# Another order of the steps in the attention part of a fused tokenizer, attention and MLP kernel

## The chip, the core and the metric

The kernel runs on one core of a Trainium2 chip. The metric is device time in microseconds (us) of one execution; of several runs the median is given. The engines are called PE (TensorE), DVE (VectorE), ACT (ScalarE), POOL (GpSimd) and SP (SyncE), as the profile calls them.

## What is computed

The reference takes 32 images and 32 texts. Each image is cut into 196 patches of 768 numbers, and the 128 text vectors are put behind them: 324 rows of 256 numbers. Then come causal attention with 16 heads of 16, and an MLP whose inputs and weights are rounded in blocks of 16 to a 4-bit grid (`_GRID`, `_MID`). Cut to what matters:

```python
h = patches @ W.T + b                      # 32 x 196 x 256
h = concatenate([h, txt], axis=1)          # 32 x 324 x 256
# attention: q, k, v of layernorm(h), 16 heads
att = softmax(where(mask, q @ k.T * 0.25, -inf))
h = h + (att @ v) @ Wo + bo
# MLP: fp4_linear quantises its input and its weight blockwise
x = layernorm(h)
h = h + fp4_linear(silu(fp4_linear(x, w_gate)) * fp4_linear(x, w_up), w_down)
```

## The kernel before

The kernel has two parts, one after the other. `phase_a` does the embedding, the attention and the quantising of the MLP's input and weights; `phase_b` does the MLP on 81 tiles of 128 rows. The change is in `phase_a` alone.

`phase_a` is a software pipeline over images, written by hand. `pipeline` runs `body(k)` for iterations -1 to 34 on every engine. In iteration n the kernel embeds image n+1 (`tok`, `h0`, `root`, `xn shift`, `xn`), makes q, k and v of image n (`xnT`, `qk`, `v`, `rest`, `part 1`, `last`), takes the row maxima of the scores of image n-1 (`MAX_A` for heads 0 to 7, `MAX_B` for heads 8 to 15, seven steps each) and its first two groups of exponentials (`exp 0`, `exp 1`), finishes the attention of image n-2 (`exp 2`, `exp 3`, `attend`, `turn`, `turnback`, `proj`), and normalises and quantises image n-3 (the steps that begin with `x2`). One of 33 pieces of the MLP's weights is quantised by nine small VectorE steps, `w 0` to `w 8`.

The list `STEPS` gives the order. Every engine walks through the same list and does its share of each step, in this order; instructions of an engine run strictly one behind the other, and between engines there are only semaphores. So a step's place in the list sets what it stands behind on each engine. Things that the steps below turn on:

- A score matmul for the maxima writes the PSUM tensor `maxp`, and VectorE's maximum (line 605) frees it. The scores for the exponentials go to `expp`, which ScalarE's exponential (line 828) frees. There is one of each. `linA` and `linB` are taken in turn by `xnT`, `qk`, `v`, `turn`, `turnback` and `proj`; `attp` is shared by `attend` and `neg`.
- `neg` transposes the maxima on TensorE (line 955) into `attp`, VectorE splits them into three bf16 parts (lines 616 to 623), and `neg out` sends them by three transfers from ScalarE's queue into rows of `qst` (line 816). `exp 0 0` waits for those of `neg 0`, and `exp 2 0` of the next iteration for those of `neg 1`.
- `w 7` is `w_y<-w_y,w_m` (line 663), a VectorE operation with both inputs in SBUF. `patches` copies the next patches (line 559), and GpSimd forms the low part in `patches lo` (line 54). `root` is GpSimd's power (lines 512 and 515), from which VectorE forms `xshift` (line 737) and ScalarE the normalised rows `xn` (line 843), which TensorE transposes in `xnT` at the start of the next iteration (line 911).
- `rest` (line 484) and `last` (line 490) are GpSimd's subtractions for the second and third bf16 part of q and k. SyncE stacks the parts into `qst` and `kst` with twelve transfers (line 426), which the next iteration's first scores wait for. The third part of k follows `last 1`. GpSimd also masks the exponentials (line 507), and `attend` waits for the mask.

Of the kernel before, what the change touches and what calls it, by code (L numbers as in the profile page):

```python
# [142 lines left out]
STEPS = [
    ("h0b",), MAX_A[0], ("x2 stats",), ("xnT", 0), ("attend", 1, 0), ("exp", 2, 0), MAX_A[1], ("xnT", 1), ("tok", 1),
    ("exp", 2, 1), ("attend", 1, 1), ("x2 root",), MAX_A[2], ("w", 0), ("exp", 2, 2), ("x2 shift",), ("qk", 0),
    MAX_A[3], ("exp", 2, 3), ("x2 norm",), ("attend", 1, 2), ("w", 1), ("tok", 1), MAX_A[4], ("rest", 0), ("tok", 1),
    ("x2 scale",), ("qk", 1), ("exp", 3, 0), MAX_A[5], ("qk", 2), ("attend", 2, 0), ("x2 y",), ("attend", 2, 1),
    ("attend", 2, 2), ("exp", 3, 1), ("x2 sq",), MAX_A[6], ("w", 2), ("tok", 1), ("w", 3), ("rest", 1), ("tok", 1),
    ("exp", 3, 2), ("neg", 0), ("neg out", 0), ("qk", 3), MAX_B[0], ("exp", 3, 3), ("attend", 3, 0), ("tok", 2),
    ("x2 t",), MAX_B[1], ("tok", 2), ("part 1", 0), ("w", 4), ("x2 q",), ("tok", 1), ("x2 out",), ("exp", 0, 0),  # L150
    MAX_B[2], ("tok", 1), ("exp", 0, 1), ("w", 5), ("attend", 3, 1), ("attend", 3, 2), MAX_B[3], ("exp", 0, 2),
    ("turn", 0), ("turn", 1), ("tok", 1), ("exp", 0, 3), ("part 1", 1), ("h0",), ("turn", 2), ("root",),
    ("exp", 1, 0), ("attend", 0, 0), ("last", 0), ("v", 0), ("exp", 1, 1), MAX_B[4], ("turnback", 0), ("v", 1),
    MAX_B[5], ("patches",), ("attend", 0, 1), ("w", 6), ("turnback", 1), ("attend", 0, 2), ("last", 1), MAX_B[6],
    ("patches lo",), ("w", 7), ("exp", 1, 2), ("v", 2), ("xn shift",), ("neg", 1), ("neg out", 1), ("proj", 0),
    ("xn",), ("exp", 1, 3), ("w", 8), ("proj", 1),
]
# [1224 lines left out]
```

## Time and profile before

| | us |
|---|---|
| median of 3 runs | 2053.52 (2045.04 to 2055.91) |
| time of the profiled execution | 2044.34 |
| span of the profiled execution | 2042.5 |
| PE busy (share of the span) | 1781.4 (87%) |
| DVE busy | 1627.8 (80%) |
| ACT busy | 961.4 (47%) |
| POOL busy | 872.1 (43%) |

The span is what the trace covers, 1.8 us less than the time of the same execution. Busy time counts instructions and no waiting.

### The profile page before, as it was taken

Reading aid. Unit: us, or ns where it says so; the run is one execution under the profiler, and the core shown is the slowest. Engines: PE = TensorE matmul, PEld = TensorE weight load, DVE = VectorE, ACT = ScalarE, POOL = GpSimd, SP = SyncE. Lnnn points to the kernel's source line nnn. Section 1 sums busy time; section 2 is a strip of 40 time slices with the busy share of each in tenths; the row PEclk is TensorE's granted clock in tenths of the full one; section 3 lists DMA queues with packets and bytes.
Section 4 is the critical chain, followed back from the end, with each engine's and each line's share of the span. In section 5 each row is a group of like instructions: output and inputs, shape, how many; then the busy total and the mean of one; then the engine's idle time right before and its main releaser. Section 6 shows DMA issues by size and latency. Waiting matters only on the chain. (4 is left out here: it accounts for less than half of the span.)

```text
span 2042.5 us, 37905 instructions
## 1 busy us (share of the span) xinstructions
PE 1781.4 (87%) x14552; PEld 1471.4 (72%) x14552; DVE 1627.8 (80%) x3188; ACT 961.4 (47%) x1646; POOL 872.1 (43%) x971
## 2 busy tenths in 40 slices
PE   3698888988888888888888888887499999999998
PEld 3477666776666766666776676664389999999997
DVE  5667788777887778877788787875399999999998
ACT  1255555555555555455554565554233333333333
POOL 5445555555555555555555555552012121121211
PEclk8899999899998999999999899997699999999999
DMA  3544554445544455444554445540211111111111
GB/s 104 92 70 71 91 87 94 81 71 90 88 90 85 71 88 87 86 93 71 87 91 86 89 71 88 78 75 21 66 52 58 58 57 60 58 60 58 60 58 47
DMA packets 140650, 152.45 MB, mean 75 GB/s; under 512 B 20279, under 2 KB 135607, under 8 KB 140471
## 3 DMA queue, kind: packets, MB, share of 16 engines
q1 hardware_dynamic: 133558, 149.02, 37.4%
q8 instruction: 117, 1.92, 0.4%
q10 hardware_dynamic: 6912, 1.00, 0.3%
q14 instruction: 63, 0.51, 0.1%
HBM read 51.25 MB, written 34.01 MB: 42 GB/s over the span
## 5 line engine op out<-in xcount | busy, mean ns | idle before, releaser
L605 DVE TENSOR_REDUCE maxima<-maxp 108x2 f32<-108x648 f32 (+2 forms) x448 | 415.6, 928 | 235.9 <-PE maxp L946 235.8
L828 ACT ACTIVATE probs<-expp 108x648 f32<-108x648 f32 (+2 forms) x512 | 363.7, 710 | 271.0 <-PE expp L971 257.3
L507 POOL TENSOR_SCALAR_AFFINE_SELECT probs<-probs 108x216 f32<-108x216 f32 (+1 forms) x512 | 286.4, 563 | 381.1 <-ACT probs L828 380.2
L1189 POOL TENSOR_TENSOR hq<-q_b,scale_b 128x704 f32<-128x704 f32 x81 | 112.6, 1390 | 471.0 <-DVE q_b L1246 471.0
L943 PE MATMUL maxp<-kst,qst 96*108 96x108 bf16 (+2 forms) x1536 | 279.6, 275 | 18.3 <-DMA kst<-parts 10.8
L971 PE MATMUL expp<-qst,kst 99*108 99x324 bf16 (+2 forms) x1536 | 251.8, 274 | 44.2 <-DMA qst<-negparts 33.8
L943 PEld LDWEIGHTS maxp<-kst,qst 96*108 96x108 bf16 x1536 | 179.1, 137 | 71.4 <-issue 23.5
L971 PEld LDWEIGHTS expp<-qst,kst 99*108 99x108 bf16 x1536 | 151.1, 134 | 106.4 <-DMA qst<-negparts 43.4
L992 PE MATMUL attp<-probs,vblk 108*32 108x324 f32 (+2 forms) x3072 | 223.2, 388 | 2.5 <-POOL probs L507 1.5
L946 PE MATMUL maxp<-mask_qk,identb 108*108 108x108 bf16 (+2 forms) x896 | 222.8, 255 | 0.0
L59 PE MATMUL gu<-wgu_hi,xqT_hi 128*128 128x512 f32 (+1 forms) x486 | 191.4, 394 | 2.0 <-DVE xqT_lo L1201 2.0
L484 POOL TENSOR_TENSOR rest<-qkf,parts 128x648 f32<-128x648 f32 x64 | 95.3, 1489 | 227.8 <-ACTq L801 227.8
L60 PE MATMUL gu<-wgu_lo,xqT_hi 128*128 128x512 f32 (+1 forms) x486 | 183.8, 378 | 0.0
L61 PE MATMUL gu<-wgu_hi,xqT_lo 128*128 128x512 f32 (+1 forms) x486 | 183.6, 378 | 0.0
L1272 ACT ACTIVATE hqT_hi<-turn_h 128x768 fp32r<-128x768 f32 x81 | 66.0, 815 | 199.2 <-PE turn_h L1339 199.2
L59 PE MATMUL tokp<-wtok_hi,patches_hi 128*88 128x256 f32 (+1 forms) x384 | 132.1, 344 | 19.1 <-POOL patches_lo L54 19.1
L843 ACT ACTIVATE xn<-h,xshift,rstd 108x256 f32<-108x256 f32 x96 | 50.6, 590 | 185.7 <-issue 175.1
L992 PEld LDWEIGHTS attp<-probs,vblk 108*32 108x32 f32 x3072 | 73.0, 113 | 75.1 <-issue 40.0
L946 PEld LDWEIGHTS maxp<-mask_qk,identb 108*108 108x108 bf16 x896 | 121.6, 136 | 1.2
L490 POOL TENSOR_TENSOR parts<-rest,parts 128x648 bf16<-128x648 f32 x64 | 113.0, 1766 | 0.0
L1262 ACT ACTIVATE silu_b<-gu 128x704 f32<-128x704 f32 x81 | 61.8, 763 | 108.2 <-PE gu L61 108.2
L60 PE MATMUL tokp<-wtok_lo,patches_hi 128*88 128x256 f32 (+1 forms) x384 | 112.5, 293 | 0.0
(183 smaller groups left out, 4499.6 us busy)
## 6 DMA issues: line engine op xcount, KB each, us to landing
qst<-parts SPq DMA_DIRECT2D x192, 162.0 KB, 5.1
kst<-parts SPq DMA_DIRECT2D x192, 162.0 KB, 5.9
patches<-in_xT SPq DMA_DIRECT2D x32, 588.0 KB, 4.6
h_dram<-h_rows SPq DMA_DIRECT2D x32, 324.0 KB
xq_dram<-x_n SPq DMA_DIRECT2D x32, 324.0 KB
xq<-xq_dram SPq DMA_DIRECT2D x81, 128.0 KB, 2.0
res<-h_dram SPq DMA_DIRECT2D x81, 128.0 KB, 2.1
out_rows<-ot SPq DMA_DIRECT2D x81, 128.0 KB, 1.7
```

The source lines that it names most:

```text
L59: pe.matmul(dst, a[0], b[0], start=start, stop=False)
L60: pe.matmul(dst, a[0], b[1], start=False, stop=False)
L61: return pe.matmul(dst, a[1], b[0], start=False, stop=stop)
L490: pool.tensor_tensor(parts[:, 2, t], rest[:, t], parts[:, 1, t], ALU.subtract).then_inc(part_done[2], 1)
L507: pool.affine_select(out=at, in_=at, compare_op=ALU.is_ge, fill=0.0, base=0, pattern=[[0, nh], [1, CH]], channel_multiplier=-1).then_inc(p ...
L605: dve.tensor_reduce(rowmax[half][:, h:h + nh, c].rearrange("p (a h) -> p a h", a=2), src, AX.X, ALU.max).then_inc(maxp_free, 1)
L828: act.activation(dst, expp[0:CH, 0:banks, 0:per * w], ACT.Exp, scale=SCALE).then_inc(expp_free, 1)
L943: pe.matmul(maxp[0:CH, a, x * w:(x + 1) * w], qst[other][0:ROWS, h, c * CH:(c + 1) * CH], kst[other][0:ROWS, h, 0:w], start=x == 0, stop=F ...
L946: ins = pe.matmul(maxp[0:CH, a, 0:per * w].rearrange("p (h w) -> p h w", w=w)[:, :, w - CH:w], identb[0:CH, 0:CH], mask_qk[:].unsqueeze(1) ...
L971: ins = pe.matmul(expp[0:CH, a, x * w:(x + 1) * w], kst[s][0:ROWS + NPART, h, kc * CH:(kc + 1) * CH], qst[s][0:ROWS + NPART, h, kc * CH:T] ...
L992: ins = pe.matmul(attp[VW * x:VW * (x + 1), kc * CH:T], v_of[:, kc, 4 * q + x, :], probs[:, q, lo:lo + T - CH * kc], start=kc == 0, stop=k ...
L1189: pool.tensor_tensor(blocks(hq[t % 2][:, 0:FF]), blocks(q[:]), spread(scale[:], P, NB_H), ALU.mult).then_inc(hq_done, 1)
```

## The change

Only the list `STEPS` changes. The same steps stand in it, each once, in another order.

```diff
 STEPS = [
-    ("h0b",), MAX_A[0], ("x2 stats",), ("xnT", 0), ("attend", 1, 0), ("exp", 2, 0), MAX_A[1], ("xnT", 1), ("tok", 1),
...
+    ("x2 stats",), MAX_A[0], ("tok", 1), ("x2 root",), ("xnT", 0), ("attend", 1, 0), ("exp", 2, 0), MAX_A[1],
...
-    ("patches lo",), ("w", 7), ("exp", 1, 2), ("v", 2), ("xn shift",), ("neg", 1), ("neg out", 1), ("proj", 0),
-    ("xn",), ("exp", 1, 3), ("w", 8), ("proj", 1),
+    MAX_B[6], ("exp", 1, 2), ("attend", 0, 2), ("v", 2), ("w", 6), ("neg", 1), ("xn",), ("neg out", 1), ("w", 7),
+    ("proj", 0), ("w", 8), ("proj", 1), ("exp", 1, 3),
 ]
```

What this does to the engines is seen in their instructions. First VectorE, near the end of an iteration in the middle of the program, from the copy of the patches on. Before:

```order
L559 CAST patches_hi<-patches 128x1176
L661 SCALAR_TENSOR_TENSOR w_y<-w_y,w_m 128x128
L54 TENSOR_TENSOR attnT_lo<-linA,attnT_hi 128x324
L605 TENSOR_REDUCE maxima<-maxp 108x2
L663 TENSOR_TENSOR w_y<-w_y,w_m 128x128
L629 TENSOR_TENSOR vblk<-linB,bv 108x16x16
L737 SCALAR_TENSOR_TENSOR xshift<-meanvar,rstd 108x3
L616 TENSOR_SCALAR negparts<-attp 24x108
L618 SCALAR_TENSOR_TENSOR negrest<-attp,negparts 24x108
L621 CAST negparts<-negrest 24x108
L623 TENSOR_TENSOR negparts<-negrest,negparts 24x108
L596 TENSOR_TENSOR h_rows<-linA,h0b 108x512
```

And after the change, the same place, from `xn shift` on:

```order
L737 SCALAR_TENSOR_TENSOR xshift<-meanvar,rstd 108x3
L54 TENSOR_TENSOR attnT_lo<-linA,attnT_hi 128x324
L605 TENSOR_REDUCE maxima<-maxp 108x2
L629 TENSOR_TENSOR vblk<-linB,bv 108x16x16
L661 SCALAR_TENSOR_TENSOR w_y<-w_y,w_m 128x128
L616 TENSOR_SCALAR negparts<-attp 24x108
L618 SCALAR_TENSOR_TENSOR negrest<-attp,negparts 24x108
L621 CAST negparts<-negrest 24x108
L623 TENSOR_TENSOR negparts<-negrest,negparts 24x108
L663 TENSOR_TENSOR w_y<-w_y,w_m 128x128
L596 TENSOR_TENSOR h_rows<-linA,h0b 108x512
```

`w 7` (line 663) stood ahead of the last eviction of v, of `xshift` and of the maxima's parts, and now stands behind them all; `xshift` has moved ahead of the last maximum.

GpSimd, from `root` (lines 512 and 515) to the next iteration's first masks. Before:

```order
L512 TENSOR_TENSOR vareps<-meanvar,eps 108x3
L515 TENSOR_TENSOR rstd<-vareps,minus_half 108x3
L507 AFFINE_SELECT probs<-probs 108x2x108
L490 TENSOR_TENSOR parts<-rest,parts 128x648
L507 AFFINE_SELECT probs<-probs 108x2x108
L490 TENSOR_TENSOR parts<-rest,parts 128x648
L54 TENSOR_TENSOR patches_lo<-patches,patches_hi 128x1176
L507 AFFINE_SELECT probs<-probs 108x4x108
L507 AFFINE_SELECT probs<-probs 108x432
L529 TENSOR_TENSOR h0b<-h_1,bo 108x768
```

And after, from `last 0` (line 490) on:

```order
L490 TENSOR_TENSOR parts<-rest,parts 128x648
L512 TENSOR_TENSOR vareps<-meanvar,eps 108x3
L515 TENSOR_TENSOR rstd<-vareps,minus_half 108x3
L54 TENSOR_TENSOR patches_lo<-patches,patches_hi 128x1176
L507 AFFINE_SELECT probs<-probs 108x2x108 x2
L490 TENSOR_TENSOR parts<-rest,parts 128x648
L507 AFFINE_SELECT probs<-probs 108x4x108
L507 AFFINE_SELECT probs<-probs 108x432
L519 TENSOR_TENSOR x_vareps<-x_meanvar,eps 108x3
```

`patches lo` (line 54) has moved from behind `last 1` to right behind `root`, ahead of `last 1`; `h0b` (line 529) no longer stands here but some masks into the next iteration.

ScalarE, from the exponential that `exp 1 2` issues at the end of an iteration. Before:

```order
L828 ACTIVATE probs<-expp 108x864
L816 DMA qst<-negparts 1x24x108 x3
L843 ACTIVATE xn<-h_1,xshift,rstd 108x256 x3
L828 ACTIVATE probs<-expp 108x432
L784 ACTIVATE xnT_hi<-linA 128x324
```

And after:

```order
L828 ACTIVATE probs<-expp 108x864
L810 ACTIVATE attT<-attp 128x324
L843 ACTIVATE xn<-h_1,xshift,rstd 108x256 x3
L816 DMA qst<-negparts 1x24x108 x3
L828 ACTIVATE probs<-expp 108x432
L784 ACTIVATE xnT_hi<-linA 128x324
```

The rows `xn` now stand ahead of the three transfers, and the copy of `attend 0`'s result (line 810) has come in behind the exponential.

In the first half of the iteration `qk 3` has moved ahead of `neg 0` and two `tok` steps behind it, `x2 norm` stands ahead of `exp 3 0` as before, `x2 t` (line 707) stands right behind the maxima's parts of `neg 0` and ahead of `MAX_B[0]`, and `h0b` stands behind `MAX_A[4]`. SyncE's list is not written by `STEPS`, but each of its transfers waits for a step: the texts' for `h0b`, the stacks' for `exp 3 3`, `part 1` and `last`.

## Rows read from the trace of the kernel before

**Rows 1.** Windows of the execution: each engine's busy time, TensorE's granted clock, DMA.

```profile
80.00:1400.00 1320.00, 1150.62 (x10541) 902.34 (x10540) 1031.03 (x2170) 712.57 (x1261) 713.26 (x835) 0.93 0.47 82
...
1470.00:2042.00 572.00, 560.98 (x3564) 513.10 (x3564) 523.09 (x893) 215.16 (x325) 112.59 (x81) 0.99 0.18 56
```

**Rows 2.** TensorE's timeline: start, length, line, tile, count, [idle <- releaser].

```profile
143.71 0.47 PE L911 MATMUL linA<-ident,xn 108*128 108x108 f32 x3 [2.58 <-ACT xn L843]
...
1293.21 0.78 PE L911 MATMUL linA<-ident,xn 108*128 108x108 f32 x3 [2.66 <-ACT xn L843]
...
1332.90 0.47 PE L911 MATMUL linA<-ident,xn 108*128 108x108 f32 x3 [1.39 <-ACT xn L843]
```

**Rows 3.** TensorE's timeline from 713 to 763 us.

```profile
713.77 0.28 PE L955 MATMUL attp<-ident,maxima 108*128 108x108 f32 x1
...
720.18 0.48 PE L971 MATMUL expp<-qst,kst 99*108 99x324 bf16 x2 [1.05 <-DMA qst<-negparts]
...
736.04 0.37 PE L59 MATMUL linB<-wo_hi,attnT_hi 128*108 128x256 f32 x1 [1.24 <-DVE vblk L629]
...
740.41 0.77 PE L911 MATMUL linA<-ident,xn 108*128 108x108 f32 x3 [2.65 <-ACT xn L843]
...
742.36 0.79 PE L971 MATMUL expp<-qst,kst 99*108 99x324 bf16 x2
...
745.15 0.44 PE L971 MATMUL expp<-qst,kst 99*108 99x324 bf16 x2
...
762.38 0.48 PE L971 MATMUL expp<-qst,kst 99*108 99x324 bf16 x2 [1.05 <-DMA qst<-negparts]
```

**Rows 4.** VectorE's timeline near 732 us, and line 663's minimum, median, maximum (ns).

```profile
731.88 0.83 DVE L605 TENSOR_REDUCE maxima<-maxp 108x2 f32<-108x648 f32 x1
...
732.62 3.04 DVE L663 TENSOR_TENSOR w_y<-w_y,w_m 128x128 f32<-128x128 f32 x1
...
L663 DVE TENSOR_TENSOR w_y<-w_y,w_m x33: 276/3030/3534, 29.2 to 1366.6; 128x128 f32<-128x128 f32 x33
```

**Rows 5.** Timelines of VectorE (first row) and GpSimd (the others).

```profile
730.60 0.76 DVE L559 CAST patches_hi<-patches 128x1176 fp32r<-128x1176 f32 x1
...
727.75 0.85 POOL L515 TENSOR_TENSOR rstd<-vareps,minus_half 108x3 f32<-108x3 f32 x1
...
728.91 1.42 POOL L490 TENSOR_TENSOR parts<-rest,parts 128x648 bf16<-128x648 f32 x1
...
730.62 2.23 POOL L490 TENSOR_TENSOR parts<-rest,parts 128x648 bf16<-128x648 f32 x1
...
732.81 2.70 POOL L54 TENSOR_TENSOR patches_lo<-patches,patches_hi 128x1176 fp32r<-128x1176 f32 x1
```

**Rows 6.** ScalarE's timeline and queue, and two of its grouped lines (500 to 1300 us).

```profile
714.38 2.27 ACTq L816 DMA_DIRECT2D qst<-negparts  x3
...
731.11 0.44 ACT L810 ACTIVATE attT<-attp 128x324 f32<-128x324 f32 x1
...
731.96 0.89 ACT L828 ACTIVATE probs<-expp 108x864 f32<-108x864 f32 x1 [0.41 <-PE expp L971]
...
736.30 2.28 ACTq L816 DMA_DIRECT2D qst<-negparts  x3
...
738.69 1.58 ACT L843 ACTIVATE xn<-h,xshift,rstd 108x256 f32<-108x256 f32 x3 [5.83 <-issue]
...
L828 ACT ACTIVATE probs<-expp 108x648 f32<-108x648 f32 (+2 forms) x300 | 213.1, 710 | 152.4 <-PE expp L971 146.9 <-issue 0.4
...
L795 ACT ACTIVATE qkf<-linB,bqk 128x324 f32<-128x324 f32 x37 | 19.7, 532 | 37.9 <-issue 37.7
```

**Rows 7.** SyncE's queue: the last stack transfer; TensorE: the first scores behind it.

```profile
732.88 0.55 SPq L426 DMA_DIRECT2D kst<-parts  x1
...
736.84 0.36 PE L943 MATMUL maxp<-kst,qst 96*108 96x108 bf16 x4
```

**Rows 8.** A window of two microseconds, columns as in the first group.

```profile
738.00:740.00 2.00, 0.00 (x0) 0.00 (x0) 2.00 (x5) 1.31 (x3) 0.00 (x0) 0.56 0.30 87
```

More of the change, by code:

```diff
@@ L143 @@
 STEPS = [
-    ("h0b",), MAX_A[0], ("x2 stats",), ("xnT", 0), ("attend", 1, 0), ("exp", 2, 0), MAX_A[1], ("xnT", 1), ("tok", 1),
[L145 to L153, printed above, removed]
@@ L154 @@
-    MAX_B[5], ("patches",), ("attend", 0, 1), ("w", 6), ("turnback", 1), ("attend", 0, 2), ("last", 1), MAX_B[6],
-    ("patches lo",), ("w", 7), ("exp", 1, 2), ("v", 2), ("xn shift",), ("neg", 1), ("neg out", 1), ("proj", 0),
-    ("xn",), ("exp", 1, 3), ("w", 8), ("proj", 1),
+    ("x2 stats",), MAX_A[0], ("tok", 1), ("x2 root",), ("xnT", 0), ("attend", 1, 0), ("exp", 2, 0), MAX_A[1],
+    ("xnT", 1), ("attend", 1, 1), ("exp", 2, 1), ("attend", 1, 2), MAX_A[2], ("x2 shift",), ("exp", 2, 2), ("qk", 0),
@@ new lines @@
+    MAX_A[3], ("tok", 1), ("exp", 2, 3), ("w", 0), ("x2 norm",), ("tok", 1), ("w", 1), MAX_A[4], ("h0b",),
+    ("x2 scale",), ("exp", 3, 0), ("qk", 1), ("qk", 2), MAX_A[5], ("x2 y",), ("exp", 3, 1), ("attend", 2, 0),
+    ("rest", 0), ("qk", 3), MAX_A[6], ("w", 2), ("attend", 2, 1), ("attend", 2, 2), ("x2 sq",), ("exp", 3, 2),
+    ("neg", 0), ("x2 t",), ("neg out", 0), ("tok", 1), ("rest", 1), MAX_B[0], ("tok", 1), ("exp", 3, 3), ("tok", 2),
+    ("tok", 2), ("part 1", 0), MAX_B[1], ("attend", 3, 0), ("tok", 1), ("x2 q",), ("exp", 0, 0), ("w", 3), ("w", 4),
@@ new lines @@
+    MAX_B[2], ("tok", 1), ("exp", 0, 1), ("x2 out",), ("attend", 3, 1), ("w", 5), ("attend", 3, 2), MAX_B[3],
+    ("exp", 0, 2), ("turn", 0), ("tok", 1), ("h0",), ("exp", 0, 3), ("v", 0), ("turn", 1), ("last", 0), ("root",),
+    ("patches",), ("patches lo",), ("part 1", 1), ("attend", 0, 0), ("exp", 1, 0), MAX_B[4], ("turn", 2),
+    ("exp", 1, 1), ("v", 1), MAX_B[5], ("turnback", 0), ("last", 1), ("xn shift",), ("turnback", 1), ("attend", 0, 1),
+    MAX_B[6], ("exp", 1, 2), ("attend", 0, 2), ("v", 2), ("w", 6), ("neg", 1), ("xn",), ("neg out", 1), ("w", 7),
```

## The prediction

> **What bounds the kernel now.** I began with the windows [rows 1]. The MLP part, from 1470 us on, has TensorE busy 561 of 572 us, and the change doesn't touch it. In the attention part TensorE is busy 1151 of 1320 us, VectorE 1031, at a mean granted clock of 0.93: no engine is full, so a chain of waits sets the time. The transposes at the start of an iteration give its period: from 143.71 to 1293.21 us there are 27 periods, 42.57 us each [rows 2].
>
> Then I followed TensorE through one iteration [rows 3]. I count from the first scores of `exp 0 0`, at 720.18. The next landmark is `exp 2 0` at 742.36, 22.2 us later, and the next `exp 0 0` comes at 762.38, 20.0 us later still. TensorE idles 1.05 us for the transfers of the maxima's parts, 1.24 us for the last eviction of v, and 2.65 us for the rows `xn`. Behind the last two its clock falls: it is granted 0.56 in the window from 738 us [rows 8], between its two levels of 1.2 and 2.4 GHz. The steps from 742.36 to 745.15 take 2.8 us; the same four steps at full clock take about 1.5 us by the pitch of such steps later in this trace (my estimate).
>
> Both waits have one source [rows 4]. Line 663 takes 3.04 us at 732.62, where its shortest instance takes 0.28, and the median of 33 is 3.03. While it stands there GpSimd runs `patches lo`, 2.70 us from 732.81 [rows 5]. Behind line 663 on VectorE are the eviction of v, `xshift` and the maxima's parts. Behind those parts on ScalarE's queue are the three transfers, 2.28 us of issue, and only then `xn` at 738.69 [rows 6]. That is the chain of the idle 2.65 us.
>
> One iteration near the end of the pipeline shows what its absence is worth: the one that ends at 1332.90 has no patches to load, so no `patches lo`. Its wait for `xn` is 1.39 us in place of 2.66, and its period is 39.69 [rows 2], 2.9 under the mean. It also leaves out the copy of the patches, so not all of this is the collision.
>
> The Trainium skill (SBUF — State Buffer, "SBUF: two separate sides") has a rule for this: a VectorE operation with two SBUF inputs, or in a 2-port mode, and a GpSimd operation exclude each other for a whole instruction. By that rule the trace agrees, with 3.04 us against 0.28.
>
> **The change, part by part: second half of the iteration.** Time T runs from `exp 0 0`. VectorE has nearly the same set of steps before the last maximum as before, so that maximum still begins at about T = 11.7 (731.88 less 720.18) [rows 3, 4]. Likewise the exponential of `exp 1 2` begins at about 11.8 (731.96) and takes 0.89, to 12.7. Behind it now stands the copy of `attend 0` (0.44), which frees `attp` at 13.1 [rows 6]. `neg 1` needs that tensor, so it can't transpose before 13.1, although the maxima are there at 12.5. Line 663 is behind it, where GpSimd has only masks: it should take 0.3 us, not 3.0, and nothing on the path stands behind it but the residuals.
>
> `xn` runs on ScalarE from 13.1 to 14.6 (1.58) [rows 6]. TensorE has `proj 0`, `proj 1`, `exp 1 3`, the first maxima and one `tok` before it needs `xn`, about 3.9 us by the pitch of these steps at full clock, so it asks at 17 or later: the wait for `xn`, 2.65 us now, goes. What is late next are the transfers of `neg 1`. They now stand behind `xn`, and the queue takes them when the last of its three pieces has been issued, at about 14.0. From the start of such a group to the scores that wait for it there are 5.8 us (714.38 to 720.18) [rows 3, 6]. So `exp 2 0` comes at 14.0 + 5.8 = 19.8, in place of 22.2. The gain is **2.4 us**.
>
> A second limit lies close. On GpSimd `last 1` now stands behind `root`, `patches lo` and two masks. The next patches are copied at about T = 7.5 to 8.2, `root` ends by 8.4, `patches lo` takes 2.7 to 11.1, two masks 0.8, and `last 1` 1.42 [rows 5], to 13.3. Before, its transfer was issued at 12.7 (732.88), and the scores that need it ran at 736.84, 3.96 us later, without a wait [rows 7]. So the first maxima may begin at about 17.2 at the latest, and `exp 2 0`, with 2.2 us of steps between, at 19.4. It doesn't decide, but only 0.4 us are between.
>
> **First half.** S runs from `exp 2 0`. TensorE no longer sits idle for 2.65 us in a piece, so I expect the clock to stay up, which takes the 1.3 us from its first steps. But the end of this half is then set by ScalarE. Up to the copy of `attend 2`, which frees `attp` for `neg 0`, it has six exponentials, `x2 norm` (three pieces, as `xn`, 1.58), four evictions of q and k at two activations each, and three short copies. With 710 and 532 ns for one [rows 6], less some 0.1 us of overlap between neighbours, that is 10.4 us. It waits some 0.5 us at first and 1.3 us for scores, so `neg 0` is at S = 12.3. The move of `qk 3` in front of it is what makes ScalarE the limit: of the evictions one (0.95) is new there. From `neg 0` to the next `exp 0 0` are now 6.4 us (713.77 to 720.18) [rows 3], all latency, and the two `tok` behind it only fill the wait. So S ends at 18.7, in place of 20.0: **1.3 us** less.
>
> The rest moves at no price: `tok` steps wait for nothing in either place. The small steps of the weight are 0.2 to 0.3 us each, and lie in VectorE's waits for scores. `x2 t` ahead of `MAX_B[0]` delays that maximum by about 0.9 us, and four `tok` between it and `MAX_B[1]` cover this; without them it would cost 0.9. `h0b`, moved past six masks of GpSimd, makes SyncE send the texts some 8 us later, but `h0` wants them half an iteration after that; the text transfers hold no others back, as the stacks' wait for `exp 3 3` is later still. The next piece of weights and the next patches are asked for at the same point of SyncE's list, behind `proj 1` and `w 8`.
>
> **The sum.** 19.8 + 18.7 = 38.5 us against 42.57. What the walk can't see goes on top. The copy of the patches and `root` now come at nearly the same time. A pair of this kind is in the trace: the copy (0.76) and GpSimd's subtraction begin within 0.02 us of each other, and GpSimd's takes 2.23 in place of 1.42, 0.81 more [rows 5]; the copy lost nothing. Of `root` (0.85) [rows 5] no row shows such a pair. If the copy wins, `patches lo` is 0.8 late and `xshift` meets it, about 0.6 on the path; if `root` wins, VectorE is 0.9 late and all behind it. From below it is nothing, from above 1.0. I take 0.7 for this and for small gaps: a period of **39.2 us**, 3.4 less. With 28 full iterations and the partial ones at the ends counted as one, that is 29 × 3.4 = 98 us. The profiled execution took 2044.3 us (its span 2042.5), 9 under the median of 2053.5, so it would take 1946. On the scale of the median I predict **1955 us**.
>
> By the skill's rule of the exclusive pair alone `root` holds VectorE's copy off for all of its time. By that the sum would be 0.3 us a period longer than mine, 1964 us.
>
> **The rivals.**
> 1. As forecast, periods of 38.7 to 40.2 give 1941 to 1985 us; chance 0.52. For it speaks that both idle pieces have one source, and the source is moved away.
> 2. Part of it is lost (0.22): the collisions come back in smaller form (`xshift`, a VectorE operation on SBUF, now stands near `patches lo` and `last 1`, up to 1.4 us), or TensorE's clock still falls, as three idle pieces of about 1 to 1.5 us remain, and costs again 1.3 us or more. `root` holding off the copy, 0.9 a period, is one of these. Periods of 40.2 to 41.9 give 1985 to 2034 us, 2009 in the middle. Against it: the idle 1.05 us at 719 left the clock at full.
> 3. More is gained (0.08): if the transfers of the maxima's parts land sooner than the 5.8 us, which would need less of the stacks' traffic beside them. Each such wait is some 1.5 us in my walk, so both gone would leave about 37 us a period: 29 × 5.6 = 162, 1891 us.
> 4. No change (0.07): another wait of the same length takes the place. Periods of 42.2 to 42.9 give 2043 to 2063 us.
> 5. Slower (0.11): GpSimd's queue decides. `last 1` stands behind `patches lo`, and the next iteration's first scores wait for its transfer. This begins to set the time when `last 1` ends 0.4 us later than worked out above, and the iteration is as long as before when it ends 4.4 us later (TensorE then reaches `exp 2 0` at 23.9 in place of 19.8). If GpSimd loses its turns to VectorE and ends 6.4 us late, each iteration has 2 us more than before: 2053.5 + 58 = 2112 us.
>
> **How the numbers follow.** A measurement of this kernel tells changes of about 0.5% (10 us) from none. Faster by more: 0.52 + 0.22 + 0.08 = 0.82; within: 0.07; slower: 0.11. The range goes from 1915 to 2030. It leaves out most of cases 3, 4 and 5, about 0.2 together with the far ends of the others, and takes in the bounds of the unknown cost (nothing to 1.0 a period is 1935 to 1964) and a clock that still falls.
>
> **What would show it.** Line 663 at 0.3 us in nearly every instance. No wait for `xn` at line 911. In its place a wait of some 1 to 2 us at line 971 for `qst<-negparts` twice in an iteration, at `exp 2 0` too, and perhaps a short one for `kst<-parts` at line 943. Periods of line 911 near 39 us, and a mean granted clock above 0.93 in the attention part. TensorE waiting a little for ScalarE's copy of `attend` ahead of both transposes at line 955. The prediction is wrong if the wait at line 943 is the long one, if line 559 or 737 has grown to over 1 us, or if the clock still falls once in an iteration.

## The result and the profile after

The changed kernel takes 1943.89 us (median of four runs, 1941.54 to 1948.95); the kernel before took 2052.78 beside it (four runs, 2045.04 to 2055.91). The ratio is 0.949, with a 95% interval of 0.946 to 0.951: 109 us less, where I had forecast 98 against 2053.5. Its profiled execution has a span of 1940.4 us against 2042.5, so the two traces differ by 102 us.

Windows of the changed kernel, columns as in [rows 1]:

```profile
80.00:1340.00 1260.00, 1137.84 (x10727) 872.85 (x10725) 991.79 (x2217) 718.01 (x1284) 723.17 (x849) 0.97 0.52 87
1370.00:1940.00 570.00, 560.36 (x3560) 513.48 (x3559) 522.21 (x890) 213.15 (x323) 112.75 (x81) 0.99 0.18 56
```

The MLP part is as before. In the attention part the granted clock has risen from 0.93 to 0.97. The next rows are three VectorE lines of the changed kernel (minimum, median and maximum in ns):

```profile
L663 DVE TENSOR_TENSOR w_y<-w_y,w_m x33: 271/273/291, 32.7 to 1262.4; 128x128 f32<-128x128 f32 x33
L737 DVE SCALAR_TENSOR_TENSOR xshift<-meanvar,rstd x32: 296/1432/3977, 29.9 to 1218.5; 108x3 f32<-108x3 f32 x32
L621 DVE CAST negparts<-negrest x64: 203/204/206, 78.7 to 1301.7; 24x108 bf16<-24x108 f32 x64
```

Line 663, 3.03 us in the median before [rows 4], takes 0.27 in every instance. But line 737, which forms `xshift` from three numbers a row, now takes 1.43 us in the median. The collision has got smaller and changed its victim.

One iteration in the middle of the changed kernel, TensorE's timeline, as in [rows 3]:

```profile
687.60 0.44 PE L911 MATMUL linA<-ident,xn 108*128 108x108 f32 x3
688.65 0.48 PE L971 MATMUL expp<-qst,kst 99*108 99x324 bf16 x2
...
701.26 0.31 PE L955 MATMUL attp<-ident,maxima 108*128 108x108 f32 x1
707.48 0.48 PE L971 MATMUL expp<-qst,kst 99*108 99x324 bf16 x2 [0.93 <-DMA qst<-negparts]
...
721.33 0.28 PE L955 MATMUL attp<-ident,maxima 108*128 108x108 f32 x1 [0.80 <-DVE maxima L605]
724.76 0.40 PE L943 MATMUL maxp<-kst,qst 96*108 96x108 bf16 x4 [0.76 <-DMA kst<-parts]
725.93 0.44 PE L911 MATMUL linA<-ident,xn 108*128 108x108 f32 x3
726.98 0.48 PE L971 MATMUL expp<-qst,kst 99*108 99x324 bf16 x2
```

The waits for `xn` and for the eviction of v are gone. From `exp 2 0` (688.65) to `exp 0 0` (707.48) are 18.83 us, and on to the next `exp 2 0` (726.98) 19.50. The period by line 911 is 38.33 us; the mean over the 27 periods from 147.79 to 1188.15 us is 38.53, because four are 39.4 to 40.2 long. Before it was 42.57 over the same number [rows 2]. At `exp 2 0` nothing waits for the transfers of `neg 1` in this iteration. What TensorE waits for near the end of the second half is `kst<-parts` at line 943, the stack's last transfer.

The four long periods have two causes. In three of them, of 39.4 us each, `exp 2 0` does wait for the transfers of `neg 1`, by 0.98, 1.21 and 1.13 us. In the fourth, of 40.2, TensorE waited 1.44 us at `exp 0 0`, and then the clock was at 1.2 GHz in the window from 592 us. A row of the first kind, and that window:

```profile
533.35 0.48 PE L971 MATMUL expp<-qst,kst 99*108 99x324 bf16 x2 [0.98 <-DMA qst<-negparts]
...
592.00:594.00 2.00, 2.00 (x14) 1.54 (x16) 1.17 (x2) 0.46 (x1) 0.37 (x1) 0.50 1.11 115
```

What leads up to the wait for `kst<-parts`. GpSimd and SyncE's queue in the changed kernel:

```profile
713.38 1.41 POOL L490 TENSOR_TENSOR parts<-rest,parts 128x648 bf16<-128x648 f32 x1
714.75 0.98 POOL L512 TENSOR_TENSOR vareps<-meanvar,eps 108x3 f32<-108x3 f32 x1
...
716.64 2.73 POOL L54 TENSOR_TENSOR patches_lo<-patches,patches_hi 128x1176 fp32r<-128x1176 f32 x1
719.65 0.37 POOL L507 TENSOR_SCALAR_AFFINE_SELECT probs<-probs 108x216 f32<-108x216 f32 x1
720.00 1.42 POOL L490 TENSOR_TENSOR parts<-rest,parts 128x648 bf16<-128x648 f32 x1
...
721.44 0.55 SPq L426 DMA_DIRECT2D kst<-parts  x1
```

And VectorE and ScalarE:

```profile
714.91 0.76 DVE L559 CAST patches_hi<-patches 128x1176 fp32r<-128x1176 f32 x1
...
718.58 1.46 DVE L737 SCALAR_TENSOR_TENSOR xshift<-meanvar,rstd 108x3 f32<-108x3 f32 x1
...
720.37 0.82 DVE L605 TENSOR_REDUCE maxima<-maxp 108x2 f32<-108x648 f32 x1
...
722.67 0.27 DVE L663 TENSOR_TENSOR w_y<-w_y,w_m 128x128 f32<-128x128 f32 x1
...
701.90 2.31 ACTq L816 DMA_DIRECT2D qst<-negparts  x3
...
720.47 1.58 ACT L843 ACTIVATE xn<-h,xshift,rstd 108x256 f32<-108x256 f32 x3
721.95 2.28 ACTq L816 DMA_DIRECT2D qst<-negparts  x3
```

There are two collisions. The small step of `root` at 714.75 (line 512) takes 0.98 us beside the copy of the patches; its median in the kernel before is 0.19. The copy itself takes 0.76, as before [rows 5]. Then `patches lo` runs from 716.64 to 719.37 and the masks to 720.02, and `xshift`, begun at 718.58, ends at 720.04: it seems to be held by the masks too. So the last maximum begins at T = 12.9, and the stack's last transfer is issued at T = 13.96, both counted from 707.48.

The gain in three pieces: the 27 steady periods gave 1149.50 - 1040.36 = 109.1 us, and 7 went back at the ends. Four of these lie ahead of 147.79 us, where the first `exp 0 0` of the program waits 6.38 us for the transfers in the new order (the kernel before waits 1.07 us there, at 82.67):

```profile
88.27 0.79 PE L971 MATMUL expp<-qst,kst 99*108 99x324 bf16 x2 [6.38 <-DMA qst<-negparts]
```

### The profile page after: what moved, and what is told of

Same layout as the page of the kernel before. It is cut to its first block and busy times, and to the rows that moved or that the text cites. A ratio compares the mean times of both kernels' runs of the same rounds, so it can differ in the third digit from the quotient of the medians.

```text
span 1940.4 us, 37904 instructions
## 1 busy us (share of the span) xinstructions
PE 1744.7 (90%) x14552; PEld 1428.4 (74%) x14552; DVE 1568.3 (81%) x3188; ACT 953.6 (49%) x1646; POOL 875.3 (45%) x971
## 5 line engine op out<-in xcount | busy, mean ns | idle before, releaser
L507 POOL TENSOR_SCALAR_AFFINE_SELECT probs<-probs 108x216 f32<-108x216 f32 (+1 forms) x512 | 295.4, 580 | 504.3 <-ACT probs L828 502.2
L943 PE MATMUL maxp<-kst,qst 96*108 96x108 bf16 (+2 forms) x1536 | 270.9, 269 | 42.1 <-DMA kst<-parts 34.6
L971 PE MATMUL expp<-qst,kst 99*108 99x324 bf16 (+2 forms) x1536 | 245.8, 270 | 52.2 <-DMA qst<-negparts 40.6
L943 PEld LDWEIGHTS maxp<-kst,qst 96*108 96x108 bf16 x1536 | 167.0, 131 | 98.5 <-DMA kst<-parts 38.6
L971 PEld LDWEIGHTS expp<-qst,kst 99*108 99x108 bf16 x1536 | 137.3, 131 | 135.6 <-DMA qst<-negparts 57.2
L946 PE MATMUL maxp<-mask_qk,identb 108*108 108x108 bf16 (+2 forms) x896 | 218.0, 249 | 0.0
L992 PE MATMUL attp<-probs,vblk 108*32 108x324 f32 (+2 forms) x3072 | 213.5, 367 | 0.0
L61 PE MATMUL tokp<-wtok_hi,patches_lo 128*88 128x256 f32 (+1 forms) x384 | 109.2, 284 | 0.0
L59 PEld LDWEIGHTS gu<-wgu_hi,xqT_hi 128*128 128x128 f32 x486 | 92.6, 191 | 16.9 <-DVE xqT_lo L1201 2.5
L484 POOL TENSOR_TENSOR rest<-qkf,parts 128x648 f32<-128x648 f32 x64 | 90.5, 1414 | 30.1 <-ACTq L801 30.1
```

The lines of the kernel that those rows point to most:

```text
L59: pe.matmul(dst, a[0], b[0], start=start, stop=False)
L61: return pe.matmul(dst, a[1], b[0], start=False, stop=stop)
L507: pool.affine_select(out=at, in_=at, compare_op=ALU.is_ge, fill=0.0, base=0, pattern=[[0, nh], [1, CH]], channel_multiplier=-1).then_inc(p ...
L943: pe.matmul(maxp[0:CH, a, x * w:(x + 1) * w], qst[other][0:ROWS, h, c * CH:(c + 1) * CH], kst[other][0:ROWS, h, 0:w], start=x == 0, stop=F ...
L946: ins = pe.matmul(maxp[0:CH, a, 0:per * w].rearrange("p (h w) -> p h w", w=w)[:, :, w - CH:w], identb[0:CH, 0:CH], mask_qk[:].unsqueeze(1) ...
L971: ins = pe.matmul(expp[0:CH, a, x * w:(x + 1) * w], kst[s][0:ROWS + NPART, h, kc * CH:(kc + 1) * CH], qst[s][0:ROWS + NPART, h, kc * CH:T] ...
```

## The experiments

All ratios are to the kernel before, run on the same chip beside them. In what follows S is the time from `exp 2 0` to `exp 0 0`, T from there to the next `exp 2 0`, each the median over 24 to 27 iterations of TensorE's timeline. Before: S 20.07, T 22.22. Changed: S 18.83, T 19.50.

### Only line 663 away from patches lo

```diff
-    ("patches lo",), ("w", 7), ("exp", 1, 2), ("v", 2), ("xn shift",), ("neg", 1), ("neg out", 1), ("proj", 0),
+    ("patches lo",), ("exp", 1, 2), ("v", 2), ("xn shift",), ("neg", 1), ("neg out", 1), ("w", 7), ("proj", 0),
```

> The kernel before, with w 7 (line 663) alone moved behind neg out 1. Theory A, a collision with patches lo whoever comes: the next VectorE operation with both inputs in SBUF is then xshift (line 737), which asks at about 733.1 while GpSimd's patches lo runs from 732.81 to 735.5. It takes the wait over: line 663 drops to 0.3 us, line 737 grows to some 2.4 us, the parts of the maxima start at about 735.7 in place of 736.0, and the period falls by 0.3 to 0.6 us: 10 to 20 us in all, ratio 0.990 to 0.995. Theory B, the place of line 663 is the cause by itself: 2.7 us fewer on the chain, so 75 to 100 us less, ratio 0.95 to 0.965, and line 737 stays at 0.2 us.

Measured: 2019.45 us, ratio 0.986 (0.980 to 0.991), nearer to the first theory; most periods are 41.0 to 41.2; S 20.10, T 21.23. Rows of two VectorE lines of this kernel, then of the timelines of VectorE, GpSimd and TensorE:

```profile
L663 DVE TENSOR_TENSOR w_y<-w_y,w_m x33: 271/273/277, 31.7 to 1341.7; 128x128 f32<-128x128 f32 x33
...
L737 DVE SCALAR_TENSOR_TENSOR xshift<-meanvar,rstd x32: 146/2517/2615, 29.2 to 1299.0; 108x3 f32<-108x3 f32 x32
...
636.37 2.50 DVE L737 SCALAR_TENSOR_TENSOR xshift<-meanvar,rstd 108x3 f32<-108x3 f32 x1
...
636.15 2.70 POOL L54 TENSOR_TENSOR patches_lo<-patches,patches_hi 128x1176 fp32r<-128x1176 f32 x1
...
643.23 0.47 PE L911 MATMUL linA<-ident,xn 108*128 108x108 f32 x3 [2.77 <-ACT xn L843]
```

The wait for line 663 is gone, and the next VectorE step on SBUF, `xshift`, stands in its place for 2.50 us (0.15 in its shortest instance). TensorE's wait for `xn` hasn't moved (2.65 before [rows 3]). The prediction booked both of TensorE's waits on line 663; moving this line alone gives 1.0 us of T.

### Only xshift and xn early

```diff
-    MAX_B[5], ("patches",), ("attend", 0, 1), ("w", 6), ("turnback", 1), ("attend", 0, 2), ("last", 1), MAX_B[6],
+    MAX_B[5], ("xn shift",), ("patches",), ("attend", 0, 1), ("w", 6), ("turnback", 1), ("attend", 0, 2), ("last", 1), MAX_B[6],
...
-    ("patches lo",), ("w", 7), ("exp", 1, 2), ("v", 2), ("xn shift",), ("neg", 1), ("neg out", 1), ("proj", 0), ("xn",),
+    ("patches lo",), ("w", 7), ("exp", 1, 2), ("v", 2), ("xn",), ("neg", 1), ("neg out", 1), ("proj", 0),
```

> The kernel before, with w 7 where it was, and xshift moved ahead of the patches' copy and xn ahead of neg 1. It tests the rival that xn standing behind the three transfers on ScalarE is what cost the time. Theory A: line 663 still takes 3.0 us, the maxima's parts and their transfers stay at 736.3, and exp 2 0, now at 742.36, can come 5.0 to 5.8 us behind them: 0.3 to 1.0 us a period less, 10 to 30 us in all, ratio 0.985 to 0.995; the wait at line 911 for xn goes and one at line 971 for qst<-negparts comes. Rival: the wait for xn was the loss, so 2.65 us a period, 77 us, ratio 0.963.

Measured: 1994.46 us, ratio 0.970 (0.964 to 0.976), more than the first theory gives and near the rival's 0.963, which lies just outside the interval; S 20.24, T 20.60. Timelines of VectorE, ScalarE's queue and TensorE:

```profile
573.88 3.06 DVE L663 TENSOR_TENSOR w_y<-w_y,w_m 128x128 f32<-128x128 f32 x1
...
577.47 2.29 ACTq L816 DMA_DIRECT2D qst<-negparts  x3
...
581.93 0.48 PE L971 MATMUL expp<-qst,kst 99*108 99x324 bf16 x2 [1.82 <-DMA qst<-negparts]
```

Here the collision stays whole, and still the kernel gains twice what the first experiment gave. And this is the place where the transfers of `neg 1` do decide: `exp 2 0` starts 4.46 us behind the start of their issue (577.47 to 581.93), where the prediction took 5.8 from `neg 0`'s place. Over the steady iterations of this trace the same stretch is 3.7 to 5.6 us long. The wait costs the clock too: in 19 of 29 first halves the granted clock is 0.92 or less and S is 20.1 to 23.1, in the other ten it is 1.00 and S is 18.6 to 18.9.

### Both, in the kernel before

The two diffs above together.

> Both edits on the kernel before: w 7 behind neg out 1, xshift ahead of the patches' copy, xn ahead of neg 1. patches lo still stands behind last 1, at 732.8 to 735.5, and what VectorE does there on SBUF alone is now two small operations of the maxima's parts (lines 621 and 623, 24x108). Theory A: these collide as well, one of them takes over 2 us, the transfers of part 1 and 2 leave at about 735.9, exp 2 0 comes at about 740.2: 2 us a period less, 55 to 65 us, ratio 0.968 to 0.975. Theory B, only the large operations collide: exp 2 0 at 738.5, 3.9 us a period less, 113 us, ratio 0.945.

Measured: 1896.66 us, ratio 0.925 (0.921 to 0.929), much faster than either theory had it, and 2.4% faster than the changed kernel. S 19.15, T 18.30. Timelines of GpSimd, VectorE, ScalarE's queue and TensorE:

```profile
583.48 2.72 POOL L54 TENSOR_TENSOR patches_lo<-patches,patches_hi 128x1176 fp32r<-128x1176 f32 x1
...
584.43 1.83 DVE L621 CAST negparts<-negrest 24x108 bf16<-24x108 f32 x1
...
586.29 1.50 ACTq L816 DMA_DIRECT2D qst<-negparts  x2
...
589.04 0.48 PE L971 MATMUL expp<-qst,kst 99*108 99x324 bf16 x2 [0.16 <-DMA qst<-negparts]
```

Again `patches lo` finds a victim: the parts' own cast of 24 rows takes 1.83 us instead of 0.20. It costs at most the 0.16 us that TensorE waits here, for the last two transfers of `neg 1` are issued at 586.29 and the scores that need them run 2.75 us later. (In seven of 28 iterations this wait is 0.4 to 0.9 us.) So a collision costs what stands behind it on the path. Run again, five times:

> The version of before with w 7 late, xn shift ahead of the patches and xn ahead of neg 1, once more and in five rounds, as the version that beats both kernels: 1891 to 1902 us, ratio 0.920 to 0.929, periods of 37.3 to 37.7.

1899.96 us (1896.63 to 1904.51), ratio 0.927 (0.924 to 0.929), as expected.

### The old order of xn and the transfers put back

The diff is that of the version with both, but `xn` stays behind the transfers.

```diff
-    ("exp", 1, 2), ("v", 2), ("xn",), ("neg", 1), ("neg out", 1), ("w", 7), ("proj", 0),
+    ("exp", 1, 2), ("v", 2), ("neg", 1), ("neg out", 1), ("w", 7), ("proj", 0), ("xn",),
```

> Before, with w 7 behind neg out 1 and xn shift ahead of the patches, but xn left behind the three transfers. It tells the place of xshift from the order of xn and the transfers on ScalarE. Theory (the order on ScalarE counts by itself): the transfers issue from about 583.5 to 586 on the scale of the version with xn ahead of them, xn runs to about 588 to 589.5, and TensorE waits for it some 1.3 to 2 us at line 911; periods 38.8 to 39.3 against 37.5, 1935 to 1950 us, ratio 0.944 to 0.952. Rival (only VectorE's lateness counted; the parts' transfers land so fast that the order on ScalarE is worth nothing): periods of 37.4 to 37.9, 1895 to 1910 us, ratio 0.924 to 0.932.

Measured: 1974.34 us, ratio 0.964 (0.961 to 0.966), slower than both theories had it. S 20.24, T 19.98. T is 1.7 us longer than with `xn` first, as the first theory had it. The rest is TensorE's clock: the granted clock between 110 and 1190 us is 0.96, and 1.00 in the version with `xn` first. Two iterations of this kernel, TensorE's waits at the start and then windows of two microseconds:

```profile
175.54 0.40 PE L943 MATMUL maxp<-kst,qst 96*108 96x108 bf16 x4 [0.60 <-DMA kst<-parts]
...
178.38 0.47 PE L911 MATMUL linA<-ident,xn 108*128 108x108 f32 x3 [1.87 <-ACT xn L843]
...
214.93 0.40 PE L943 MATMUL maxp<-kst,qst 96*108 96x108 bf16 x4 [1.38 <-DMA kst<-parts]
...
216.96 0.47 PE L911 MATMUL linA<-ident,xn 108*128 108x108 f32 x3 [1.06 <-ACT xn L843]
```

```profile
176.00:178.00 2.00, 0.51 (x6) 0.24 (x4) 2.00 (x5) 1.35 (x3) 0.00 (x0) 1.00 0.12 32
178.00:180.00 2.00, 1.62 (x16) 0.98 (x17) 1.67 (x7) 1.11 (x4) 1.29 (x2) 1.00 0.89 233
...
216.00:218.00 2.00, 1.04 (x11) 0.45 (x11) 1.98 (x4) 1.67 (x4) 0.70 (x2) 1.00 0.68 203
218.00:220.00 2.00, 2.00 (x14) 1.86 (x11) 0.76 (x5) 0.71 (x1) 2.00 (x2) 0.50 0.87 230
```

Both iterations idle about 2.5 us in the two places. In the first the clock stays at 2.4 GHz and the period is 38.58 us; in the second it is at 1.2 GHz (0.50) from 218 us, and the period is 40.36. The next one, from 257.32, has waits of 0.60 and 1.86 us, as the first has, and its clock falls. So the same idle time doesn't always cost the clock.

### The collision put back into the changed kernel

```diff
-    ("patches",), ("patches lo",), ("part 1", 1), ("attend", 0, 0), ("exp", 1, 0), MAX_B[4], ("turn", 2),
...
+    ("patches",), ("part 1", 1), ("attend", 0, 0), ("exp", 1, 0), MAX_B[4], ("turn", 2), ("exp", 1, 1), ("v", 1),
+    MAX_B[5], ("turnback", 0), ("last", 1), ("xn shift",), ("turnback", 1), ("w", 6), ("attend", 0, 1), MAX_B[6],
+    ("patches lo",), ("w", 7), ("exp", 1, 2), ("attend", 0, 2), ("v", 2), ("neg", 1), ("xn",), ("neg out", 1),
```

`w 6`, `patches lo` and `w 7` leave their places of the changed kernel.

> The kernel after, with patches lo moved back behind the last maximum, w 6 moved ahead of attend 0 1 and w 7 behind patches lo, so ahead of the last eviction of v and of neg 1, as they stood before; xshift and xn stay early. last 1 then ends some 2.7 us sooner, so the stack transfer no longer limits. Theory A: line 663 takes 1.5 to 2.5 us again, neg 1 is done some 0.6 to 1.3 us later than in the kernel after, and exp 2 0 with it: a period of 38.9 to 39.7, ratio to the kernel before 0.957 to 0.967 (the kernel after has 0.949). If the whole gain hung on the collision alone, the ratio would go back to about 1.

Measured: 2011.70 us, ratio 0.981 (0.976 to 0.985): some 3% slower than the changed kernel, twice as much as expected, and not in the way expected. S 19.23, T 21.68. VectorE, GpSimd and TensorE:

```profile
636.71 2.55 DVE L737 SCALAR_TENSOR_TENSOR xshift<-meanvar,rstd 108x3 f32<-108x3 f32 x1
...
636.56 2.68 POOL L54 TENSOR_TENSOR patches_lo<-patches,patches_hi 128x1176 fp32r<-128x1176 f32 x1
...
640.80 0.28 PE L955 MATMUL attp<-ident,maxima 108*128 108x108 f32 x1 [2.13 <-DVE maxima L605]
```

SyncE, GpSimd and VectorE don't run in the list's order against each other: GpSimd came to `patches lo` earlier than VectorE to line 663, and met `xshift`, which in the changed order stands ahead of the last maximum. Line 663 took 0.28. So this run doesn't give the price of line 663 in its old place. It shows a collision of 2.6 us ahead of a maximum, and T 2.2 us longer than in the changed kernel. A part of that is the clock: in 28 of 29 iterations the granted clock of T is 0.92, against 1.00 in nearly all of the changed kernel. How much the maximum behind the collision costs by itself isn't shown, since three steps moved.

### The two limits of the second half, one at a time and together

The changed kernel once more, for its noise; then with `xshift` behind the last maximum; then with the subtraction of k's third part (`last 1`) ahead of `patches lo`; then with both.

> The kernel after, unchanged, as the yardstick on the same chip for the three below: periods of 38.3 us, ratio 0.949 to the kernel before, line 737 (xshift) at 1.4 us, a wait of 0.7 to 1.0 us for kst<-parts at line 943 and one of 0.8 us for the maxima at line 955 in nearly every iteration.

```diff
-    MAX_B[5], ("turnback", 0), ("last", 1), ("xn shift",), ("turnback", 1), ("attend", 0, 1), MAX_B[6],
+    MAX_B[5], ("turnback", 0), ("last", 1), ("turnback", 1), ("attend", 0, 1), MAX_B[6], ("xn shift",),
```

> The kernel after with xshift moved behind the last maximum, so that it no longer stands ahead of it while GpSimd's patches lo runs. Theory S, the stack's last transfer sets the second half: line 737 falls to 0.5 us or less and the wait of 0.8 us for the maxima at line 955 goes, but last 1 ends when it did, so the wait for kst<-parts at line 943 grows by the same 0.6 to 0.8 us and the period stays within 0.15 us of 38.3; ratio within 0.004 of the yardstick. Theory N, neg 1 sets it: 0.65 us a period less, 19 us, ratio 0.009 lower.

```diff
-    ("patches",), ("patches lo",), ("part 1", 1), ("attend", 0, 0), ("exp", 1, 0), MAX_B[4], ("turn", 2),
+    ("patches",), ("part 1", 1), ("last", 1), ("patches lo",), ("attend", 0, 0), ("exp", 1, 0), MAX_B[4], ("turn", 2),
...
-    MAX_B[5], ("turnback", 0), ("last", 1), ("xn shift",),
+    MAX_B[5], ("turnback", 0), ("xn shift",),
```

> The kernel after with last 1 and then patches lo moved behind part 1 1, so that GpSimd does the last part of k some 2 us sooner and patches lo 1.4 us later. Theory S with the collision: the wait for kst<-parts at line 943 goes, but patches lo now runs from about 718.1 to 720.8 on the time scale of the after trace, and xshift, asked for at 718.6, takes some 2.2 us in place of 1.4; neg 1 is 0.8 us later. One wait takes the place of the other and the period stays within 0.25 us of 38.3. If the stack's transfer alone set the time, the period would fall by 0.7 to 0.9 us, 20 to 26 us in all.

> Both edits on the kernel after: last 1 ahead of patches lo, and xshift behind the last maximum. Theory: each alone only hands the wait on, both together take it away: exp 2 0, at 726.98 on the time scale of the after trace, comes at about 725.6, a period of 36.9 to 37.3, 30 to 42 us less than the kernel after, ratio to the kernel before 0.928 to 0.935. If the two edits were independent and additive, this would be the sum of the two runs above, near nothing by my own expectations for them.

| | us | ratio | S | T |
|---|---|---|---|---|
| changed, again | 1949.17 | 0.951 (0.948 to 0.954) | 18.83 | 19.50 |
| xshift late | 1961.00 | 0.956 (0.952 to 0.959) | 18.83 | 19.55 |
| last 1 first | 1965.82 | 0.959 (0.956 to 0.963) | 19.31 | 19.28 |
| both | 1923.36 | 0.938 (0.934 to 0.942) | 19.42 | 17.82 |

Alone, neither edit gains. A row of each on TensorE's timeline, `xshift` late first:

```profile
578.20 0.40 PE L943 MATMUL maxp<-kst,qst 96*108 96x108 bf16 x4 [1.53 <-DMA kst<-parts]
```

```profile
580.67 0.28 PE L955 MATMUL attp<-ident,maxima 108*128 108x108 f32 x1 [1.54 <-DVE maxima L605]
```

In the changed kernel TensorE waits twice in this stretch, 0.80 for the maximum and 0.76 for `kst`. With the first cause removed it waits 1.53 for the second, and the other way round 1.54 for the first (`xshift` takes 2.20 us there, at 577.18). T moves by 0.05 and 0.2. With both removed T falls by 1.7, and S rises by 0.6; together 1.1 us a period are gained (periods of 37.2 to 37.3, as expected, and a ratio just above the expected 0.928 to 0.935). The two limits end within some tenths of a microsecond of each other, so neither shows by its wait what it is worth.

Both single edits are even slower than the changed kernel in the median; for `xshift` late the two intervals overlap. Between 110 and 1200 us the clock fell once in the trace of the changed kernel and never in that of its repeat, but four times with `xshift` late and ten times with `last 1` first. Most of these falls come behind the one wait of 1.5 us or more, but most such waits have no fall behind them, one of 2.11 us included. With `xshift` late three periods are 42.4 to 43.0 long, nearly all others 38.2 to 39.5. Two of the three have the fall behind that wait (1.52 and 1.82 us); the third has it at a wait of 2.43 us for the transfers of `neg 0`. TensorE in the first of them, windows of that kernel:

```profile
266.00:268.00 2.00, 2.00 (x11) 1.79 (x10) 0.27 (x1) 0.71 (x1) 0.38 (x1) 0.50 0.73 254
...
272.00:274.00 2.00, 2.00 (x9) 1.92 (x8) 0.76 (x2) 0.89 (x1) 0.57 (x1) 0.50 0.00 0
```

The clock is at 1.2 GHz from 266 to 274 us (and 0.74 and 0.70 in the windows on either side), behind a wait of 1.52 us at 263.20, and this period is some 4.5 us longer than its neighbours.

### The halves of the program swapped

First, the order of before up to `exp 0 0`, and the changed one behind it:

```diff
-    ("x2 stats",), MAX_A[0], ("tok", 1), ("x2 root",), ("xnT", 0), ("attend", 1, 0), ("exp", 2, 0), MAX_A[1],
...
+    ("h0b",), MAX_A[0], ("x2 stats",), ("xnT", 0), ("attend", 1, 0), ("exp", 2, 0), MAX_A[1], ("xnT", 1), ("tok", 1),
...
     ("exp", 0, 0), ("w", 3), ("w", 4), MAX_B[2], ("tok", 1), ("exp", 0, 1), ("x2 out",), ("attend", 3, 1),
```

> The changed kernel's order from exp 0 0 on, with the order of before ahead of it. Theory (nearly all of the gain lies in the second half; the first half got shorter because the clock stays up, not by its own reorder): in the version of before with w 7 late and xn early, the old first half took 19.07 us from exp 2 0 to exp 0 0 (551.72 to 570.79), the changed one takes 18.83 in the changed kernel. So periods of 38.5 to 38.8 against 38.35, about 6 us more in all: 1940 to 1958 us, ratio to before 0.946 to 0.955. Rival (the reorder of the first half is worth the 1.3 us a period that the prediction gave it): periods of 39.5 or more, 1975 us or more, ratio 0.963 or more.

Measured: 1937.31 us, ratio 0.945 (0.942 to 0.948), periods of 38.4; S 19.26, T 19.13. The reorder of the first half is worth nothing here: it makes S 0.4 shorter and T 0.4 longer.

Second, the changed order up to `exp 0 0`, and behind it that of the version with both edits:

```diff
-    MAX_B[5], ("turnback", 0), ("last", 1), ("xn shift",), ("turnback", 1), ("attend", 0, 1), MAX_B[6],
...
+    MAX_B[5], ("xn shift",), ("patches",), ("attend", 0, 1), ("w", 6), ("turnback", 1), ("attend", 0, 2), ("last", 1),
+    MAX_B[6], ("patches lo",), ("exp", 1, 2), ("v", 2), ("xn",), ("neg", 1), ("neg out", 1), ("w", 7), ("proj", 0),
```

> The changed kernel's order up to exp 0 0, and behind it the order of the version of before with w 7 late and xn early (xshift ahead of the copy of the patches, patches lo behind the last maximum). Theory (the halves are independent): 18.83 + 18.25 = 37.1 us a period, against 37.5 in that version: 11 us less than its 1897 in all, 1880 to 1892 us, ratio 0.917 to 0.923. Rival (the halves are tied, since the stack's transfers and the clock reach over the border): periods of 37.5 or more, 1897 us or more, ratio 0.925 or more.

Measured: 1940.11 us, ratio 0.948 (0.945 to 0.951), periods of 38.4. The halves are tied, and the theory falls: T is 18.41, near the 18.25 expected, but S is 20.02 in place of 18.83. Its VectorE, and TensorE's next maxima:

```profile
603.72 1.08 DVE L678 BATCH_NORM_STATS2 x_stats<-h_rows 108x6 f32<-108x256 f32 x3
...
605.06 1.03 DVE L605 TENSOR_REDUCE maxima<-maxp 108x8 f32<-108x864 f32 x1
...
606.14 0.39 PE L943 MATMUL maxp<-kst,qst 96*108 96x216 bf16 x2 [1.10 <-DVE maxima L605]
```

The changed order puts the statistics of the finished rows (`x2 stats`) ahead of the iteration's first maximum, and they wait for `proj 1`, which closes the other half. In the changed kernel TensorE does the scores of `exp 1 3` between `proj 1` and the first maxima and reaches the next maxima later, and does not wait; here it waits 1.10 us. That the place of the statistics is the cause wasn't tried by itself.

## Why the prediction held, step by step

The time was 11 us under the forecast, and the case was the first one: periods of 38.5 us on average, just under the 38.7 where that case begins, against 39.2 with everything on top, and 38.5 in the bare walk. One of the prediction's own signs of being wrong showed all the same: line 737 grew to over 1 us. And the wait that ends the second half is the one at line 943, though it isn't the longest (0.76 us, against 0.93 at `exp 0 0` and 0.80 at `neg 1`).

**One source of both idle pieces: half right.** The forecast named line 663 beside `patches lo`. Line 663 was cured in every instance, as forecast, but alone this gives 1.0 us of T (22.22 to 21.23), and `xn` stays as late as it was, because `xshift` takes over the collision. With `xshift` out of the way as well T goes to 19.98, and with `xn` ahead of the transfers to 18.30. In the kernel before three edits share 3.9 us of T, by 1.0, 1.25 and 1.7 us, and only the last saves the clock too (S from 20.24 to 19.15). These shares hold for this order of the edits: put last, the move of line 663 gives 2.3 us (T from 20.60 to 18.30). By the Trainium skill (SBUF — State Buffer, "SBUF: two separate sides") whichever of the two engines starts first has the shared ports for its whole instruction, and the other waits until then. By that rule the traces agree: three numbers a row (line 737) stood 2.50 us, 24 rows (line 621) 1.83 us.

**Second half, 19.8 us forecast, 19.50 measured: right by a wrong step.** The step that failed is the one on what is late next: "From the start of such a group to the scores that wait for it there are 5.8 us", and so the transfers of `neg 1` would set `exp 2 0` at 19.8. Their issue began at T = 14.47 (721.95), and `exp 2 0` at 19.50 did not wait for them, so they took less than 5.03. So it was in 24 of the 27 steady periods; in the other three `exp 2 0` waited for them and came 6.1 to 6.4 us behind the start of their issue. Where they do decide, with `xn` early in the kernel before, they take 4.46 in the row shown and 3.7 to 5.6 in all, and in the fastest version the last two take 2.75. The 5.8 came from `neg 0`, whose issue (701.90) has the stacks' transfers right behind it on SyncE's queue; there it is 5.58 still (to 707.48). That the stacks' traffic makes the difference was not tried by itself, and it leaves the spread within one place open. The half was set by what the prediction put 0.4 us below, the stack's last transfer. `last 1` ended at T = 13.94 rather than 13.3 (`root` ended at 9.2 rather than 8.4, its first step having taken 0.8 us more beside the copy), its transfer and the scores behind it took 3.32 rather than 3.96, and 2.2 us of steps follow: 13.96 + 3.32 + 2.22 = 19.50. The two errors of 0.6 cancelled, so that the bound worked out for it, 19.4, was good to 0.1 by luck; and it was luck too that the transfers' 19.8 lay so near.

**First half, 18.7 forecast, 18.83 measured: size right.** `neg 0` came at S = 12.61 in place of 12.3 (the prediction's own terms, 10.4, 0.5 and 1.3, add up to 12.2), and 6.22 us followed in place of 6.4. But the reorder isn't what shortened it. With the old first half S is 19.26, T is 19.13 and the sum is the same. What the first half gained, it gained nearly all by the clock, as the prediction had said of its first steps: S is 20.10 and 20.24 in the two versions that keep the wait for `xn`, 19.15 in the one that has both edits. The trace of before shows it too: in two of its 29 iterations the granted clock of the first half is 1.00, and there the old order took 18.9 and 19.1 us (316.65 to 335.57, and 1041.21 to 1060.30).

**Collisions, 0.7 forecast: all of it there, little seen in the period.** `root` did lose to the copy (0.98 in place of 0.19), and `xshift` did meet `patches lo`, 1.46 us in place of 0.15. That is the case "if the copy wins"; the other, `root` holding off the copy, didn't come, although GpSimd's record begins first (714.75 against 714.91). The last maximum was 1.2 us late and TensorE waited 0.80 for it. But the chain through GpSimd ended as late by itself, so the collision of `xshift` cost T nothing: without it T is 19.55. That GpSimd chain has the 0.8 us that `root` lost in it; what T would be without that collision wasn't tried. The period was 38.33, under the 38.5 of the bare walk; the mean of 38.53 holds the longer periods.

**The clock: right.** 0.97 in the attention part against 0.93; between 110 and 1200 us the clock falls once in the trace of the changed kernel, and 25 times in that of the kernel before. At `neg 1` TensorE waited for VectorE's maxima (0.80), not for ScalarE's copy as forecast. Rival 2 was present in its mechanisms (`xshift` over 1 us, TensorE waiting for line 943) and absent in its price. Of rival 3 the condition holds in most iterations, the transfers of `neg 1` land sooner than 5.8, but not its result, since the stack stands behind them. Rival 5 had the right queue: `last 1` was later than worked out by the 0.6 us that make it decide, and not by the 4.4 that would have made the kernel slower.

**The sum.** 29 periods of 3.4 gave 98 us. The traces have 27 of 4.04, 109.1, less 7 at the ends of the pipeline, which the prediction had counted as a gain of one more period. The first `exp 0 0`, with its 6.38 us, was not looked at.

What stays open: why the clock falls in one iteration and not in another with the same waits; and why the transfers of `neg 1` take a microsecond longer in some iterations. The fastest version found is the kernel before with three steps moved, 0.927 in five runs, against 0.951 for the changed kernel.

## What to carry to other kernels

When a VectorE step on SBUF is moved away from a long GpSimd one, look for the step that will stand in its place: GpSimd's instruction is still there, and here it blocked the next one in turn, down to three elements a row. Move it to where the blocked step has the least on the path behind it. When two waits stand close together on TensorE, work out both ends: one edit hands its wait to the other, and only both together gain. And take a transfer's latency from the same place in the program and from many iterations: from issue to first use these took 2.75 to 5.8 us in different places, and 3.7 to 5.6 in one place of one trace.
